# One core, eight batches of an adaLN block: new written-out step orders for five engines, and one wait less before a small load

## The chip, the cores and the metric

The kernel runs on one NeuronCore of a Trainium2 chip. The metric is the device time of one execution in microseconds (us). The time before is 694.33 us, the median of three runs (693.51 to 694.66).

## The reference

Eight batches of 1024 rows with 256 features, all float32. For each batch `b`:

```
mod = silu(c) @ wmod                       # six vectors of 256: sa, ca, ga, sb, cb, gb
ga, gb = sign * max(|.|, 0.25)
h = layernorm(x) * (1 + ca) + sa
x = x + ga * softmax((h*w_lhs) @ (h*w_rhs)^T) @ h      # 1024 x 1024 scores
h = layernorm(x) * (1 + cb) + sb
x = x + gb * (relu(h @ W1 + b1) @ W2 + b2)             # 256 -> 1024 -> 256
```

## The kernel before

A batch is cut into 8 tiles of 128 rows (two halves of 4). Every float32 product on TensorE is made of three: a value is split into a rounded part (`hi`) and a rest (`lo`), and hi*hi, hi*lo and lo*hi are added. TensorE so has the bulk of the work, and the other engines split, normalise, subtract the row maximum, exponentiate and turn blocks.

The attention of batch b and the feed-forward part (MLP) of batch b-1 run in one phase, together with the first layer norm of batch b+1. The phases are `before`, `first` (batch 0), `second` (batch 1), `middle` (a hardware loop over batches 2 to 6), `last` (batch 7) and `after` (the MLP of batch 7 alone). In each phase each engine (pe, act, dve, pool, sp) walks through a list of steps that is written out by hand as a string (`SECOND_STEPS` L70, `STEPS` L98, `LAST_STEPS` L126, `AFTER_STEPS` L151); `-` marks a step of batch b-1, `+` one of b+1. An engine runs its list strictly in order; between engines there are only semaphores. The steps that this text speaks of are:

- pe: `SC.n` the scores of row tile n (L631 to L633). They go by turns to two buffers, so SC.n waits until DVE has read SC.(n-2). `F.n` first MLP layer (L642 to L644, 6 matmuls of 512 columns), `G.n` second layer (L565, L566, L571, 12 of 256), `MB.h` spreads the row maxima of half h (L709), `AV.n` (L744 to L748, 24 matmuls) attention times values of row tile n, again in two buffers: AV.n waits until DVE has read AV.(n-2). G.0 waits for XG.3.
- dve: `SC.n` reads scores out with their maximum (L936 to L941), `ST`/`QT` turn blocks of them (L986, L994), `MX.h` row maxima, `SB.n` subtraction of the maximum (L972 to L983; it needs AV.(n-3) finished on pe), `SM.n` the rest `lo` of the exponentials (L1017), `AV.n` reads AV.n and adds it to x (L1023 to L1038, the read is L1034), `OUT.h` gates and adds the MLP result (L1132, L1136), `XG.k` writes x + gb*b2 to `x_mlp` (L1157), `VL.h` scales the values by the attention modulation `attn_mod` (L1144), `V.h` their rest (L1086), `B2`/`BH` turn normalised rows into blocks (L1096, L1097), `T2`/`TH` make the rests of the turned features (L1108; L1103, L1105).
- pool: `F.n` the rest of the hidden layer (L1194), `L1`/`L2` statistics (L1175 to L1178), `N1`/`N2` normalisation (L1185), `XC.k` adds to x (L1245).
- act: `F.n` relu and rounded part (L769, L773), `EX.n`, `SM.n` exponentials and their rounded part, `VN`, `V`, `T2`, `TH` likewise.
- sp, which issues all transfers: `AM` loads `attn_mod` (L450), `X0`/`X1` halves of x, `XT.h` the rows of the next batch's layer norm (`ln_t`, L489; XT.0 waits for B2.1), `S2`/`R2` and `SH`/`RH` store and reload blocks (L431, L438), `QW`/`QR`, `SW`/`SR` those of the scores, `GA` and `GB` two gate vectors, `O0`/`O1` the outputs (L501, L510). XG.2 waits until O1.0 and O1.1 of the batch before have landed, because it overwrites `x_mlp` (L1155).

The step that loads `gb_b2` and the step before it in the sp lists that has the same wait:

```
elif kind == "GB":
    wait(sp, xg_done, T // 2 * b)
    sp.dma_start(gb_b2[:], mod_rows[b, 3, :].partition_broadcast(P)).then_inc(gb_b2_in, 16)
elif kind == "X1":
    sp.wait_ge(xg_done, T // 2 * b)
    sp.dma_start(x_cur[:, HT:T, :], x_rows[b, 1]).then_inc(x_in[1], 16)
```

Of the kernel before, what the change touches and what calls it, by code (L numbers as in the profile page):

```python
# [148 lines left out]


AFTER_STEPS = {  # L151
    "pe": """
        F.0- F.1- F.2- F.3- F.4- F.5- G.0- G.1- G.2- G.3- F.6- G.4- G.5- F.7- F.8- F.9- F.10- G.6- G.7- F.11-
        F.12- G.8- G.9- F.13- G.10- F.14- F.15- G.11- G.12- G.13- GT.0-
    """,
    "act": """
        F.0- F.1- F.2- F.3- F.4- F.5- T2.1- F.6- F.7- F.8- F.9- F.10- F.11- F.12- F.13- F.14- F.15-
    """,
    "dve": """
        B2.1- XG.2- XG.3- T2.1- OUT.0- F.15- OT.0-  # L160
    """,
    "pool": """
        N2.1- F.0- F.1- F.2- F.3- F.4- F.5- F.6- F.7- F.8- F.9- F.10- F.11- F.12- F.13- F.14- OT.0-
    """,
    "sp": """
        S2.1- R2.1- GA.0- O0.0- O1.0- OT.2- OT.3-
# [1110 lines left out]
```

## Time and profile before

| quantity | value |
|---|---|
| time, median of three runs | 694.33 us |
| the profiled execution's own time | 694.33 us |
| its span, first to last instruction | 692.5 us |
| TensorE busy | 680.2 us (98%) |
| VectorE busy | 578.7 us (84%) |
| ScalarE busy | 428.2 us (62%) |
| GpSimd busy | 377.2 us (54%) |
| mean granted TensorE clock | 0.998 |

Busy is the sum of an engine's instructions over the span; the ends of matmuls are modelled, so TensorE's figure doesn't tell how much of its peak is used. What an engine waits for stands in brackets behind a row, with the instruction that released it. The distance between the starts of two matmuls is a better measure of a lost moment than the bracket: the bracket leaves out the time in which the earlier matmul still counts as running.

### The profile page before, as it was taken

Reading aid. Unit: us, or ns where it says so; the run is one execution under the profiler, and the core shown is the slowest. Engines: PE = TensorE matmul, PEld = TensorE weight load, DVE = VectorE, ACT = ScalarE, POOL = GpSimd, SP = SyncE. Lnnn points to the kernel's source line nnn. Section 1 sums busy time; section 2 is a strip of 40 time slices with the busy share of each in tenths; the row PEclk is TensorE's granted clock in tenths of the full one; section 3 lists DMA queues with packets and bytes.
Section 4 is the critical chain, followed back from the end, with each engine's and each line's share of the span. In section 5 each row is a group of like instructions: output and inputs, shape, how many; then the busy total and the mean of one; then the engine's idle time right before and its main releaser. Section 6 shows DMA issues by size and latency. Waiting matters only on the chain. (4 is left out here: it accounts for less than half of the span.)

```text
span 692.5 us, 13552 instructions
## 1 busy us (share of the span) xinstructions
PE 680.2 (98%) x4551; PEld 621.7 (90%) x4551; DVE 578.7 (84%) x1200; ACT 428.2 (62%) x625; POOL 377.2 (54%) x396
## 2 busy tenths in 40 slices
...
DMA packets 71744, 88.56 MB, mean 128 GB/s; under 512 B 6752, under 2 KB 62624, under 8 KB 71712
## 3 DMA queue, kind: packets, MB, share of 16 engines
...
HBM read 51.66 MB, written 36.47 MB: 127 GB/s over the span
## 5 line engine op out<-in xcount | busy, mean ns | idle before, releaser
L1194 POOL TENSOR_TENSOR hid_lo<-hid,hid_hi 128x512 fp32r<-128x512 f32 x127 | 176.5, 1397 | 184.9 <-ACT hid_hi L773 184.4
L769 ACT ACTIVATE hid<-col,b1T 128x512 f32<-128x512 f32 x128 | 86.4, 675 | 94.7 <-PE col L644 76.3
L565 PE MATMUL acc<-W2hi,hid_hi 128*128 128x256 f32 x480 | 117.4, 279 | 0.0
L566 PE MATMUL acc<-W2lo,hid_hi 128*128 128x256 f32 x480 | 116.7, 278 | 0.0
L744 PE MATMUL score<-V,Phi 128*128 128x258 f32 x448 | 109.4, 282 | 3.7 <-DVE x_cur L1034 3.1
L745 PE MATMUL score<-V,Phi 128*128 128x256 f32 x448 | 108.5, 281 | 0.0
L850 ACT ACTIVATE soft<-soft 128x1024 f32<-128x1024 f32 x56 | 59.2, 1058 | 70.2 <-DVE soft L983 48.6
L773 ACT ACTIVATE hid_hi<-hid 128x512 fp32r<-128x512 f32 x128 | 81.0, 633 | 34.8 <-PE acc L571 26.3
L642 PE MATMUL col<-h2hi,W1hi 128*128 128x512 f32 x256 | 101.3, 396 | 0.8 <-ACT hid L769 0.8
L644 PE MATMUL col<-h2hi,W1lo 128*128 128x512 f32 x256 | 100.9, 394 | 0.0
L643 PE MATMUL col<-h2lo,W1hi 128*128 128x512 f32 x256 | 100.4, 392 | 0.0
L565 PEld LDWEIGHTS acc<-W2hi,hid_hi 128*128 128x128 f32 x480 | 90.3, 188 | 1.4 <-issue 0.2
L566 PEld LDWEIGHTS acc<-W2lo,hid_hi 128*128 128x128 f32 x480 | 90.2, 188 | 1.3
L744 PEld LDWEIGHTS score<-V,Phi 128*128 128x128 f32 x448 | 85.0, 190 | 7.0 <-issue 5.9
L745 PEld LDWEIGHTS score<-V,Phi 128*128 128x128 f32 x448 | 84.1, 188 | 0.7
L571 PE MATMUL acc<-W2hi,hid_lo 128*128 128x256 f32 x480 | 77.1, 277 | 0.0
L1017 DVE TENSOR_TENSOR Plo<-soft,Phi 128x1024 fp32r<-128x1024 f32 x56 | 73.4, 1319 | 4.1 <-ACT Phi L866 4.1
L1245 POOL TENSOR_TENSOR x_cur<-x_cur,attn_mod 128x512 f32<-128x512 f32 x32 | 47.3, 1481 | 43.8 <-DVE ln_v L1144 31.8
L571 PEld LDWEIGHTS acc<-W2hi,hid_lo 128*128 128x128 f32 x480 | 64.5, 188 | 0.4
L748 PE MATMUL score<-V,Plo 128*128 128x258 f32 x448 | 63.3, 283 | 0.0
L866 ACT ACTIVATE Phi<-soft 128x1024 fp32r<-128x1024 f32 x56 | 57.7, 1051 | 0.7
L748 PEld LDWEIGHTS score<-V,Plo 128*128 128x128 f32 x448 | 57.3, 189 | 0.9 <-DVE Plo L1017 0.9
(154 smaller groups left out, 1477.3 us busy)
## 6 DMA issues: line engine op xcount, KB each, us to landing
...
```

The lines of the kernel that those rows point to most:

```text
L565: nc.tensor.matmul(o, hi, W2hi[:, it, :], start=(it == 0 and (apart or t % 2 == 0)), stop=False, skip_group_check=True)
L566: nc.tensor.matmul(o, hi, W2lo[:, it, :], start=False, stop=False, skip_group_check=True)
L571: last = nc.tensor.matmul(o, lo, W2hi[:, it, :], start=False, stop=(it == FT - 1), skip_group_check=True)
L642: nc.tensor.matmul(col[n % 2][:], W1hi[:, kk, tile], h2hi[:, kk, cols], start=(kk == 0), stop=False)
L643: nc.tensor.matmul(col[n % 2][:], W1hi[:, kk, tile], h2lo[:, kk, cols], start=False, stop=False)
L644: last = nc.tensor.matmul(col[n % 2][:], W1lo[:, kk, tile], h2hi[:, kk, cols], start=False, stop=(kk == DK - 1))
L744: nc.tensor.matmul(o, Phi[:, slot, t, :], V[:, t, 0:VW], start=(t == 0), stop=False)
L745: nc.tensor.matmul(o[:, 0:D], Phi[:, slot, t, :], V[:, t, VP:VP + D], start=False, stop=False)
L748: last = nc.tensor.matmul(o, Plo[:, slot, t, :], V[:, t, VP:VP + VW], start=False, stop=(t == T - 1))
L769: nc.scalar.activation(hid[:, n % 2, :], col[n % 2][:], ACT.Relu, bias=b1T[:, n % FT:n % FT + 1]).then_inc(col_read, 1)
L773: nc.scalar.activation(hid_hi[:, n % RING, :], hid[:, n % 2, :], ACT.Copy).then_inc(hid_hi_done, 1)
L1194: G.tensor_tensor(hid_lo[:, n % RING, :], hid[:, n % 2, :], hid_hi[:, n % RING, :].bitcast(F32), ALU.subtract).then_inc(hid_lo_done, 1)
```

## The change

The lists of `SECOND_STEPS`, `STEPS`, `LAST_STEPS` and `AFTER_STEPS` are replaced by others with the same steps in another order, for all five engines. `BEFORE_STEPS` and `FIRST_STEPS` stay. In the step GB the wait for `xg_done` is taken out; in each of the lists the step X1, which has that wait, stands ahead of GB. No instruction on tiles is added or removed. The middle phase (five of the eight batches) in full, and of the others the lists that the text speaks of:

```diff
 SECOND_STEPS = {
     "pe": """
-        SC.0 SC.1 F.0- SC.2 F.1- SC.3 F.2- SC.4 SC.5 G.0- F.3- F.4- SC.6 G.1- SC.7 F.5- G.2- G.3- G.4- MB.0
-        G.5- F.6- F.7- AV.0 F.8- F.9- G.6- F.10- G.7- AV.1 F.11- G.8- G.9- AV.2 G.10- MB.1 F.12- F.13- AV.3
-        F.14- G.11- AV.4 G.12- G.13- F.15- AV.5 AV.6 AV.7 G.14- G.15-
+        SC.0 SC.1 F.0- SC.2 SC.3 SC.4 F.1- F.2- SC.5 F.3- F.4- SC.6 SC.7 G.0- G.1- G.2- G.3- MB.0 F.5- G.4-
+        F.6- F.7- G.5- G.6- F.8- F.9- G.7- AV.0 F.10- AV.1 F.11- F.12- G.8- MB.1 AV.2 AV.3 F.13- G.9- G.10-
+        AV.4 G.11- F.14- G.12- AV.5 F.15- G.13- AV.6 G.14- G.15- AV.7
     """,
     "dve": """
-        SC.0 B2.1- XG.2- SC.1 SC.2 XG.3- VL.0 ST.0 SC.3 V.0 SC.4 SC.5 QT.0 L1.0+ ST.1 VL.1 ST.2 SC.6 SC.7
-        BH.0+ MX.0 ST.3 SB.0 T2.1- V.1 QT.1 SM.0 SB.1 AV.0 L1.1+ SM.1 SB.2 MX.1 OUT.0- AV.1 BH.1+ SM.2 SB.3
-        MX.2 TH.0+ SM.3 SB.4 SB.5 AV.2 XG.0 AV.3 SM.4 XG.1 SB.6 AV.4 B2.0 SM.5 SM.6 SB.7 TH.1+ AV.5 SM.7 AV.6
-        AV.7 OUT.1- T2.0
+        SC.0 ST.0 SC.1 B2.1- ST.1 SC.2 XG.2- VL.0 SC.3 SC.4 QT.0 L1.0+ XG.3- SC.5 V.0 SC.6 SC.7 T2.1- ST.2
+        QT.1 ST.3 MX.0 VL.1 SB.0 BH.0+ V.1 SB.1 SB.2 SM.0 L1.1+ OUT.0- MX.1 SM.1 SB.3 MX.2 AV.0 SM.2 AV.1
+        BH.1+ SB.4 SM.3 AV.2 SB.5 SB.6 AV.3 SM.4 TH.0+ SB.7 XG.0 SM.5 TH.1+ B2.0 AV.4 SM.6 AV.5 XG.1 SM.7 AV.6
+        OUT.1- AV.7 T2.0
     """,
     "sp": """
-        AM.0 S2.1- X1.0 XT.0+ R2.1- QW.0 SW.0 QR.0 SR.0 SH.0+ SW.1 XT.1+ SR.1 RH.0+ GA.0- QW.1 QR.1 SH.1+
-        O0.0- GB.0 RH.1+ S2.0 X0.0+ R2.0 O1.0- O1.1-
+        AM.0 S2.1- SW.0 XT.0+ R2.1- GA.0- QW.0 SR.0 QR.0 X1.0 SW.1 SR.1 QW.1 XT.1+ GB.0 QR.1 SH.0+ O0.0- RH.0+
+        SH.1+ RH.1+ S2.0 R2.0 O1.0- O1.1- X0.0+
     """,
...
 STEPS = {
     "pe": """
-        SC.0 SC.1 F.0- F.1- SC.2 F.2- SC.3 F.3- SC.4 G.0- SC.5 F.4- SC.6 F.5- SC.7 G.1- G.2- F.6- G.3- MB.0
-        F.7- G.4- F.8- G.5- G.6- G.7- F.9- F.10- F.11- G.8- AV.0 AV.1 G.9- G.10- G.11- F.12- MB.1 F.13- AV.2
-        AV.3 G.12- F.14- AV.4 AV.5 G.13- AV.6 G.14- F.15- AV.7 G.15-
+        SC.0 SC.1 F.0- SC.2 SC.3 F.1- F.2- SC.4 F.3- SC.5 G.0- SC.6 G.1- SC.7 F.4- G.2- F.5- F.6- G.3- G.4-
+        MB.0 F.7- G.5- G.6- AV.0 F.8- G.7- F.9- F.10- AV.1 MB.1 F.11- AV.2 F.12- AV.3 F.13- G.8- G.9- G.10-
+        AV.4 G.11- F.14- AV.5 G.12- AV.6 F.15- G.13- G.14- G.15- AV.7
     """,
     "act": """
-        F.0- VN.0 F.1- F.2- V.0 F.3- T2.1- F.4- F.5- VN.1 F.6- EX.0 SM.0 F.7- V.1 F.8- L1.0+ F.9- EX.1 EX.2
-        F.10- SM.1 F.11- TH.0+ EX.3 SM.2 SM.3 EX.4 F.12- F.13- EX.5 SM.4 SM.5 TH.1+ EX.6 SM.6 MC.0 F.14- EX.7
+        F.0- VN.0 F.1- F.2- V.0 F.3- T2.1- F.4- VN.1 F.5- V.1 F.6- EX.0 SM.0 F.7- EX.1 SM.1 EX.2 F.8- F.9-
+        L1.0+ EX.3 SM.2 F.10- SM.3 TH.0+ EX.4 SM.4 F.11- F.12- EX.5 SM.5 F.13- EX.6 SM.6 TH.1+ F.14- EX.7 MC.0
         SM.7 F.15- T2.0
     """,
     "dve": """
-        B2.1- SC.0 SC.1 XG.2- VL.0 ST.0 XG.3- SC.2 ST.1 SC.3 QT.0 SC.4 ST.2 V.0 ST.3 SC.5 L1.0+ T2.1- SC.6
-        SC.7 QT.1 MX.0 BH.0+ SB.0 VL.1 SM.0 SB.1 V.1 OUT.0- SB.2 MX.1 L1.1+ SM.1 AV.0 SB.3 AV.1 MX.2 BH.1+
-        SM.2 SM.3 SB.4 TH.0+ SB.5 AV.2 AV.3 SM.4 XG.0 SM.5 SB.6 AV.4 XG.1 B2.0 SM.6 SB.7 TH.1+ AV.5 SM.7 AV.6
-        AV.7 OUT.1- T2.0
+        XG.2- SC.0 XG.3- SC.1 B2.1- SC.2 ST.0 ST.1 SC.3 VL.0 QT.0 SC.4 L1.0+ SC.5 ST.2 ST.3 SC.6 V.0 SC.7
+        BH.0+ QT.1 T2.1- VL.1 MX.0 V.1 SB.0 SB.1 SB.2 SM.0 L1.1+ MX.1 SM.1 SB.3 MX.2 AV.0 SM.2 SB.4 OUT.0-
+        AV.1 SM.3 SB.5 TH.0+ BH.1+ AV.2 SM.4 AV.3 SB.6 SB.7 SM.5 XG.0 XG.1 SM.6 AV.4 B2.0 TH.1+ AV.5 SM.7 AV.6
+        OUT.1- AV.7 T2.0
     """,
     "pool": """
-        N2.1- XC.0 F.0- F.1- F.2- F.3- L1.0+ F.4- N1.0+ F.5- F.6- F.7- XC.1 F.8- F.9- XC.2 F.10- L1.1+ N1.1+
-        F.11- XC.3 F.12- F.13- L2.0 N2.0 F.14- F.15- L2.1
+        N2.1- F.0- XC.0 F.1- F.2- L1.0+ N1.0+ F.3- XC.1 F.4- F.5- XC.2 F.6- F.7- F.8- XC.3 F.9- F.10- L1.1+
+        N1.1+ F.11- L2.0 F.12- N2.0 F.13- F.14- F.15- L2.1
     """,
     "sp": """
-        AM.0 GA.0- S2.1- XT.0+ R2.1- SW.0 QW.0 X1.0 QR.0 SR.0 SW.1 SH.0+ QW.1 SR.1 XT.1+ RH.0+ GB.0 QR.1 O0.0-
-        SH.1+ RH.1+ S2.0 R2.0 X0.0+ O1.0- O1.1-
+        XT.0+ AM.0 X1.0 S2.1- R2.1- QW.0 GA.0- SW.0 QR.0 GB.0 SR.0 QW.1 SH.0+ SW.1 XT.1+ QR.1 SR.1 RH.0+ O0.0-
+        SH.1+ RH.1+ S2.0 R2.0 O1.0- X0.0+ O1.1-
     """,
 }
 LAST_STEPS = {
     "pe": """
-        SC.0 SC.1 F.0- SC.2 F.1- F.2- SC.3 G.0- G.1- F.3- F.4- SC.4 SC.5 G.2- G.3- SC.6 F.5- SC.7 F.6- F.7-
-        MB.0 G.4- G.5- F.8- G.6- AV.0 F.9- F.10- G.7- F.11- AV.1 AV.2 G.8- F.12- MB.1 G.9- AV.3 G.10- F.13-
-        AV.4 G.11- F.14- G.12- F.15- AV.5 AV.6 G.13- AV.7 G.14- G.15-
+        SC.0 SC.1 SC.2 F.0- SC.3 F.1- SC.4 F.2- SC.5 F.3- SC.6 SC.7 G.0- F.4- G.1- G.2- F.5- F.6- G.3- G.4-
+        MB.0 F.7- G.5- F.8- F.9- AV.0 G.6- G.7- F.10- AV.1 F.11- AV.2 MB.1 AV.3 F.12- G.8- F.13- G.9- G.10-
+        F.14- AV.4 G.11- G.12- AV.5 F.15- G.13- AV.6 G.14- G.15- AV.7
     """,
     "dve": """
-        SC.0 B2.1- ST.0 XG.2- SC.1 XG.3- ST.1 SC.2 ST.2 SC.3 QT.0 VL.0 SC.4 V.0 ST.3 SC.5 VL.1 SC.6 T2.1- SC.7
-        MX.0 SB.0 QT.1 V.1 SM.0 SB.1 AV.0 SM.1 SB.2 OUT.0- SM.2 SB.3 MX.1 MX.2 SM.3 AV.1 AV.2 SB.4 AV.3 SM.4
-        SB.5 SB.6 B2.0 SM.5 SB.7 AV.4 SM.6 XG.0 AV.5 SM.7 XG.1 AV.6 T2.0 AV.7 OUT.1-
+        SC.0 SC.1 ST.0 XG.2- VL.0 SC.2 SC.3 ST.1 XG.3- QT.0 B2.1- SC.4 SC.5 V.0 VL.1 ST.2 SC.6 ST.3 SC.7 T2.1-
+        MX.0 QT.1 V.1 SB.0 SB.1 SM.0 MX.1 SB.2 SB.3 MX.2 SM.1 AV.0 AV.1 SM.2 SM.3 OUT.0- AV.2 AV.3 SB.4 SB.5
+        SB.6 SM.4 B2.0 SM.5 SB.7 AV.4 XG.0 SM.6 SM.7 XG.1 AV.5 T2.0 AV.6 OUT.1- AV.7
     """,
...
 AFTER_STEPS = {
     "pe": """
-        F.0- F.1- F.2- F.3- F.4- F.5- G.0- G.1- G.2- G.3- F.6- G.4- G.5- F.7- F.8- F.9- F.10- G.6- G.7- F.11-
-        F.12- G.8- G.9- F.13- G.10- F.14- F.15- G.11- G.12- G.13- GT.0-
+        F.0- F.1- F.2- G.0- F.3- F.4- G.1- G.2- F.5- G.3- F.6- F.7- G.4- G.5- G.6- F.8- F.9- G.7- G.8- F.10-
+        F.11- F.12- G.9- F.13- G.10- F.14- F.15- G.11- G.12- G.13- GT.0-
     """,
     "dve": """
-        B2.1- XG.2- XG.3- T2.1- OUT.0- F.15- OT.0-
+        XG.2- XG.3- B2.1- T2.1- OUT.0- F.15- OT.0-
     """,
     "pool": """
-        N2.1- F.0- F.1- F.2- F.3- F.4- F.5- F.6- F.7- F.8- F.9- F.10- F.11- F.12- F.13- F.14- OT.0-
+        F.0- F.1- N2.1- F.2- F.3- F.4- F.5- F.6- F.7- F.8- F.9- F.10- F.11- F.12- F.13- F.14- OT.0-
     """,
...
@@ -452,7 +452,6 @@
                     elif kind == "GA":
                         sp.dma_start(gb_all[:], mod_rows[f, 2, :].partition_broadcast(P)).then_inc(gb_in, 16)
                     elif kind == "GB":
-                        wait(sp, xg_done, T // 2 * b)
                         sp.dma_start(gb_b2[:], mod_rows[b, 3, :].partition_broadcast(P)).then_inc(gb_b2_in, 16)
                     elif kind == "S2":
                         store_blocks(ph.turn(b, "T2", n))
```

## Rows read from the trace of the kernel before

**Rows 1.** the page, first part: busy us, share of the span, instructions

```profile
PE 680.2 (98%) x4551; PEld 621.7 (90%) x4551; DVE 578.7 (84%) x1200; ACT 428.2 (62%) x625; POOL 377.2 (54%) x396
```

**Rows 2.** the waits of TensorE, 71 to 700: us, times, longest

```profile
PE score L744 <- DVE x_cur L1034: 3.1, 5, 0.6
PE col L642 <- ACT hid L769: 0.8, 1, 0.8
PE score L631 <- DVE S L941: 0.7, 1, 0.7
PE score L744 <- ACT Phi L866: 0.5, 1, 0.5
```

**Rows 3.** busy us by stretch (PE, PEld, DVE, ACT, POOL), clock: batch 4

```profile
316.70:398.70 82.00, 81.29 (x563) 75.18 (x562) 74.09 (x153) 54.81 (x80) 47.14 (x48) 1.00 0.48 141
```

**Rows 4.** timeline of TensorE: start, us, what, idle before it

```profile
311.14 0.39 PE L643 MATMUL col<-h2lo,W1hi 128*128 128x512 f32 x1
311.37 0.40 PE L644 MATMUL col<-h2hi,W1lo 128*128 128x512 f32 x1
312.37 0.38 PE L744 MATMUL score<-V,Phi 128*128 128x258 f32 x1 [0.61 <-DVE x_cur L1034]
312.59 0.28 PE L745 MATMUL score<-V,Phi 128*128 128x256 f32 x1
312.71 0.28 PE L744 MATMUL score<-V,Phi 128*128 128x258 f32 x1
...
324.11 0.40 PE L644 MATMUL col<-h2hi,W1lo 128*128 128x512 f32 x1
324.61 0.50 PE L631 MATMUL score<-Rhi,Lhi 128*128 128x512 f32 x1
```

**Rows 5.** timeline of VectorE, late in batch 4: SB.7, then TH.1

```profile
389.63 0.54 DVE L972 TENSOR_TENSOR soft<-S,score 128x384 f32<-128x384 f32 x1
...
390.89 0.74 DVE L1103 SCALAR_TENSOR_TENSOR Llo<-featT,wl,Lhi 128x512 fp32r<-128x512 f32 x1
```

**Rows 6.** line L1034 (DVE's read of AV): ns min/median/max, first and last start, form

```profile
L1034 DVE SCALAR_TENSOR_TENSOR x_cur<-score,inv_sum,x_cur x56: 483/484/489, 107.9 to 642.8; 128x256 f32<-128x256 f32 x56
```

**Rows 7.** line L1017 (DVE's SM): the same columns

```profile
L1017 DVE TENSOR_TENSOR Plo<-soft,Phi x56: 1181/1224/2332, 105.2 to 636.9; 128x1024 fp32r<-128x1024 f32 x56
```

**Rows 8.** timeline of VectorE where batch 4 begins

```profile
319.61 1.53 DVE L1108 TENSOR_TENSOR h2lo<-featT,h2hi 128x512 fp32r<-128x512 f32 x2
322.26 0.71 DVE L1096 STREAM_TRANSPOSE blocks<-ln_t 128x512 f32<-128x512 f32 x1 [1.12 <-POOL ln_t L1185]
...
323.49 1.05 DVE L936 TENSOR_SCALAR_CACHE_REDUCE S<-score 128x896 f32<-128x896 f32 x1
...
325.49 0.69 DVE L1157 TENSOR_TENSOR x_mlp<-x_cur,gb_b 128x512 f32<-128x512 f32 x1
326.09 1.67 DVE L1144 SCALAR_TENSOR_TENSOR ln_v<-ln_v,rs,attn_mod 128x256 f32<-128x256 f32 x4
...
328.30 1.38 DVE L1157 TENSOR_TENSOR x_mlp<-x_cur,gb_b 128x512 f32<-128x512 f32 x1
```

**Rows 9.** the page, DMA issues: count, KB each, median us to landing

```profile
out<-x_mlp SPq DMA_DIRECT2D x15, 256.0 KB, 2.2
...
attn_mod<-mod_rows SPq DMA_DIRECT2D x8, 256.0 KB, 3.8
```

**Rows 10.** timeline of GpSimd, the same stretch

```profile
319.00 3.10 POOL L1185 TENSOR_SCALAR ln_t<-x_cur,nm,rs 128x256 f32<-128x256 f32 x4 [0.22 <-POOL rs L1178]
327.84 1.29 POOL L1245 TENSOR_TENSOR x_cur<-x_cur,attn_mod 128x512 f32<-128x512 f32 x1 [5.74 <-DVE ln_v L1144]
```

**Rows 11.** timeline of SyncE's queue, the same stretch: when a transfer is issued

```profile
318.52 1.71 SPq L510 DMA_DIRECT2D out<-x_mlp  x2
320.76 0.37 SPq L450 DMA_DIRECT2D attn_mod<-mod_rows  x1
```

**Rows 12.** timeline of GpSimd, beginning of the phase after

```profile
646.03 2.17 POOL L1185 TENSOR_SCALAR ln_t<-x_cur,nm,rs 128x256 f32<-128x256 f32 x4 [0.21 <-issue]
```

More of the change, by code:

```diff
@@ L75 @@
+        AV.4 G.11- F.14- G.12- AV.5 F.15- G.13- AV.6 G.14- G.15- AV.7
     """,
     "act": """
-        VN.0 F.0- L1.0+ V.0 F.1- F.2- VN.1 F.3- F.4- T2.1- V.1 F.5- EX.0 SM.0 F.6- F.7- EX.1 SM.1 F.8- F.9-
-        EX.2 TH.0+ SM.2 F.10- F.11- EX.3 SM.3 F.12- F.13- EX.4 EX.5 SM.4 MC.0 TH.1+ EX.6 SM.5 SM.6 F.14- EX.7
-        F.15- SM.7 T2.0
+        VN.0 F.0- F.1- F.2- V.0 T2.1- F.3- F.4- MC.0 L1.0+ VN.1 V.1 F.5- EX.0 F.6- F.7- SM.0 EX.1 EX.2 F.8-
+        F.9- SM.1 SM.2 F.10- EX.3 SM.3 TH.0+ F.11- EX.4 SM.4 F.12- EX.5 SM.5 TH.1+ EX.6 F.13- EX.7 SM.6 SM.7
@@ L80 @@
+        F.14- F.15- T2.0
     """,
     "dve": """
-        SC.0 B2.1- XG.2- SC.1 SC.2 XG.3- VL.0 ST.0 SC.3 V.0 SC.4 SC.5 QT.0 L1.0+ ST.1 VL.1 ST.2 SC.6 SC.7
-        BH.0+ MX.0 ST.3 SB.0 T2.1- V.1 QT.1 SM.0 SB.1 AV.0 L1.1+ SM.1 SB.2 MX.1 OUT.0- AV.1 BH.1+ SM.2 SB.3
-        MX.2 TH.0+ SM.3 SB.4 SB.5 AV.2 XG.0 AV.3 SM.4 XG.1 SB.6 AV.4 B2.0 SM.5 SM.6 SB.7 TH.1+ AV.5 SM.7 AV.6
-        AV.7 OUT.1- T2.0
+        SC.0 ST.0 SC.1 B2.1- ST.1 SC.2 XG.2- VL.0 SC.3 SC.4 QT.0 L1.0+ XG.3- SC.5 V.0 SC.6 SC.7 T2.1- ST.2
@@ L86 @@
+        QT.1 ST.3 MX.0 VL.1 SB.0 BH.0+ V.1 SB.1 SB.2 SM.0 L1.1+ OUT.0- MX.1 SM.1 SB.3 MX.2 AV.0 SM.2 AV.1
+        BH.1+ SB.4 SM.3 AV.2 SB.5 SB.6 AV.3 SM.4 TH.0+ SB.7 XG.0 SM.5 TH.1+ B2.0 AV.4 SM.6 AV.5 XG.1 SM.7 AV.6
+        OUT.1- AV.7 T2.0
     """,
     "pool": """
-        N2.1- F.0- XC.0 F.1- F.2- XC.1 L1.0+ F.3- N1.0+ F.4- F.5- F.6- F.7- XC.2 F.8- L1.1+ F.9- N1.1+ XC.3
-        F.10- F.11- F.12- F.13- L2.0 N2.0 F.14- F.15- L2.1
+        N2.1- XC.0 F.0- L1.0+ F.1- F.2- F.3- N1.0+ F.4- F.5- F.6- F.7- F.8- F.9- F.10- L1.1+ N1.1+ XC.1 F.11-
```

17 lines of the change are left out of this document (7 added, 10 removed).

## The prediction

> **What bounds the kernel now.** First the page: TensorE is busy 680.2 us, 98% of the span [rows 1]. No work is removed, so only TensorE's lost moments can be won. Second its waits from 71 us on [rows 2]: one reason occurs five times, once in each middle batch; three others occur once. Third the stretch of one middle batch [rows 3]: it takes 82.0 us, with VectorE busy 74.1, so VectorE is 8 us from being the bound itself. Fourth TensorE's timeline, by distances between starts [rows 4]. Two 512-column matmuls start 0.23 apart, two of 256 columns 0.12. Ahead of AV.7 the distance is 1.00, so 0.77 is lost where the bracket shows 0.61; ahead of SC.2 (324.61) it is 0.50, so 0.27 is lost where no bracket stands. A middle batch so loses 1.04 us of 82.0. For the single waits I add the same 0.16 to each: 0.86 in the second phase, 0.66 in the last, 0.96 in the phase after. Together 5 x 1.04 + 2.48 = 7.7 us: the most that new orders of the same work behind 71 us can win. What they can lose has no such ceiling.
>
> For the sums: an F step is 6 x 0.23 = 1.4 us of TensorE, a G step 12 x 0.12 = 1.4, an AV step 24 x 0.12 = 2.9. Times below are counted from TensorE's first matmul of a batch (316.7 for batch 4) and the period without losses is 82.0 - 1.04 = 81.0.
>
> **The wait ahead of AV.7 (five times 0.77).** AV.7 needs VectorE's read of AV.5. Between the end of AV.5 and AV.7 TensorE had G.13, AV.6, G.14, F.15: 3 x 1.4 + 2.9 = 7.1 us. Now it has G.12, AV.6, F.15, G.13, G.14, G.15: 9.9 us. VectorE still does TH.1 (four instructions of 0.74, the first in [rows 5]) ahead of AV.5, but XG.1, SM.6 and SB.7 no longer lie between AV.4 and AV.5 on its list. 2.8 us more time against 0.77 missing: this one goes.
>
> What is late next is AV.6, which needs the read of AV.4. From the end of AV.4 TensorE now has G.11, F.14, AV.5, G.12: 7.1 us. VectorE has SB.7 (which itself needs AV.4 finished; 1.26 by the starts in [rows 5]), SM.5 1.2, XG.0 and XG.1 0.6 each, SM.6 1.2, and the read of AV.4, 0.48 [rows 6] and 0.2 for the reciprocal ahead of it: 5.6 us. SM.6 takes between 1.2 and 2.3 [rows 7], so up to 6.7. VectorE reaches SB.7 by my count some 0.9 after AV.4's end, which gives 6.5 to 7.6 against 7.1. New loss: 0 to 0.5, taken as 0.3.
>
> **The wait ahead of SC.2 (five times 0.27).** VectorE stood 1.12 us for N2.1 ahead of B2.1, and SC.0 behind it was read late [rows 8]. Now XG.2, SC.0, XG.3, SC.1 stand ahead of B2.1. F.1 is moved behind SC.3, so TensorE wants SC.0's read at 7.65 - 1.4 = 6.25. AV.7 is now the last PE step; its own step on VectorE, reciprocal, read and two statistics, is some three times the 0.48 of the read [rows 6] and ends at 1.45, T2.0 (1.5, [rows 8]) at 2.95. XG.2 adds a wait: O1.1 must have landed. OUT.1 now stands before AV.7, G.15 being finished 2.9 us before the phase's end, so O1.1 is issued at about 0.4 and lands 2.2 later [rows 9], at 2.6; with X0's 512 KB now issued between O1.0 and O1.1 I allow 3.8, the landing time of the small load in [rows 9], which gives 4.2. Queued behind XG.2 on VectorE are SC.0 (then TensorE's SC.2), XG.3 and X1 on SyncE. XG.2 0.6 and SC.0 1.0 [rows 8] end at 4.6 to 5.8 against 6.25. The 0.27 goes; the bounds of the new loss are 0 and 0.3.
>
> XG.2 and XG.3 now run beside N2.1 on GpSimd. XG.3 took 1.38 instead of 0.69 where it started at 328.30, inside XC.0 (327.84 to 329.13) [rows 8, 10]: it ended 0.55 after XC.0 did, as if it had waited. One N2.1 instruction lasts 3.10/4 = 0.78, so one such wait puts SC.0's read at 5.4 to 6.6, the upper bound 0.35 late. The Trainium skill says it as a rule (SBUF — State Buffer, Who interferes with whom): a VectorE instruction with both inputs in SBUF and a GpSimd instruction that reads SBUF exclude each other, the second one waiting till the first is through. By that rule the move costs up to 0.35 a batch, without it nothing; the trace agrees in the row cited.
>
> **SyncE's order (AM behind XT.0).** AM was issued at 320.76 - 316.7 = 4.1 [rows 11], VL.0 used it at 9.4 [rows 8]. XT.0 now stands first, and waits until B2.1 has run. N2.1 ends about 1.45 later than before (5.4, [rows 10]), at 6.9; B2.1 ends at about 8.3; AM is issued at 8.9 and lands at 12.7 (3.8, [rows 9]). In the new list VL.0 comes after two SC, two ST and another SC, at about 12.2. So VectorE waits 0.5 here, behind it QT.0, SC.4 and XC.0 on GpSimd. TensorE meets SC.6 (which needs SC.4 read) later than that; the next meeting is MB.0, then AV.0, where my count leaves 0.3 to 0.5 us of slack. Taken as nothing; bounds 0 and 2.0, the latter if the 512 KB of XT.0 and X1 around it double its landing time.
>
> The wait removed in GB costs nothing now: X1, ahead of it, has the same wait. 0, and no bound other than 0.
>
> **Second phase.** The 0.86 is SC.5 waiting for SC.3's read behind VL.0; the new list puts one F step more between SC.3 and SC.5, and it goes. But G.0 to G.3 now run together and MB.0 comes two steps (2.8 us) earlier on TensorE, while VectorE's work ahead of MX.0 is as long as it was (VL.1 and BH.0 out; T2.1, QT.1 and ST.3 in). The 2.8 must come out of VectorE's idle time, of which a whole batch has 8 [rows 3]. New loss 0 to 2.0, taken as 1.0. Net: 0.1 lost.
>
> **Last phase.** AV.6 came directly behind AV.5 and waited for EX/SM.6 (0.66). Now F.15 and G.13 stand between, 2.8 us. It goes; 0.2 for new ones, bounds 0 and 1. Net 0.5 won.
>
> **Phase after.** N2.1 held GpSimd for 2.17 [rows 12] ahead of F.0's rest, ACT's F.2 and so TensorE's F.4 (0.96). It is moved behind F.0 and F.1, and goes. But G.0 now comes after three F steps, at 4.2, and needs XG.3: O1.1 lands at 2.6, two XG of 0.69 to 1.38 [rows 8] end at 4.0 to 5.4. Loss 0 to 1.2, taken as 0.5. Net 0.5 won. Moved N2.1 delays the turned features for F.8, which has 0 to 1 us left by the same kind of count.
>
> **Sum.** 5 x (1.04 - 0.3) - 0.1 + 0.5 + 0.5 = 4.6. The profiled execution's own time is 694.33, 1.8 outside the span, and it is also the median: 694.33 - 4.6 = 689.7.
>
> **Rivals.**
> 1. All losses go and none comes: 694.33 - 7.7 = 686.6. For it: each new wait above is at 0 at its lower bound, and VectorE has 8 us idle. Against it: VectorE then has 7.
> 2. The gains come back elsewhere (AV.6 0.5 and SC.2 0.35 a batch, and 0.2 at AV.0): 693.7 to 694.3, no change.
> 3. Slower: the attention modulation. If AM lands 2.0 later than the 12.7 counted, VL.0, SC.4, SC.6's reads and finally MX.0 and SM.0 on VectorE are 2.5 late, 0.5 of it is slack, and TensorE stands 2.0 at MB.0 or AV.0 in each middle batch: 5 x (2.0 + 0.3 - 1.04) = 6.3 lost, less 0.9 won at the ends: 699.7. From a landing at about 13.9 on (1.2 later) it outweighs the gain; at that point the time is 694 to 695. For it: three more transfers are issued within 2 us of AM. Against it: they stand behind it, except one.
>
> **How the numbers follow.** My forecast 0.48 (687.5 to 692.5), rival 1 0.20, rival 2 0.14, rival 3 0.18. A measurement of this kernel tells 0.2% (1.4 us) from no change. Faster: 0.48 + 0.20 = 0.68; same 0.14; slower 0.18. The range goes from rival 1's time to 695.5, just into rival 3; beyond that less than 0.15 is left, below it some 0.03.
>
> **What would show it.** Right: in the middle batches no wait of TensorE ahead of AV.7 for L1034, no distance over 0.23 ahead of SC.2, a period of 81.0 to 81.5, and the largest wait ahead of AV.6. VectorE's first XG.2 waits for a transfer or not at all. No wait in the phase after for L769. Wrong: a wait of TensorE for L1013 or for Plo at AV.0 (rival 3), VL.0 held by the `attn_mod` transfer for over 1.7 us; or a period of 82 with the lost time spread over new places (rival 2). A lower granted clock anywhere behind 71 us would be outside all of these.

## The result and the profile after

The changed kernel takes 735.43 us (median of four runs, 734.62 to 737.37) against 693.92 (four runs): ratio 1.060, 95% interval 1.0578 to 1.0627. I had forecast 689.7, 686.5 to 695.5. The time is outside the range and on the other side.

The page and the waits of TensorE after, to be laid beside [rows 1] and [rows 2]. Lines behind the removed wait have numbers lower by one (L708 is MB, L747 the last third of AV, L570 that of G, L1012 the row maximum, L1016 SM, L1143 VL):

```profile
PE 694.4 (94%) x4551; PEld 629.5 (85%) x4551; DVE 595.5 (81%) x1200; ACT 431.6 (59%) x625; POOL 374.5 (51%) x396
```

```profile
PE score L708 <- DVE row_max L1012: 17.3, 5, 3.8
PE score L747 <- DVE Plo L1016: 7.6, 6, 3.8
PE score L630 <- DVE S L932: 2.9, 5, 0.9
PE col L641 <- ACT hid L768: 1.9, 1, 1.9
PE col L641 <- DVE h2lo L1107: 1.5, 1, 1.5
PE score L630 <- DVE x_cur L1033: 1.4, 5, 0.3
...
PE score L743 <- DVE x_cur L1033: 0.7, 1, 0.7
```

The wait ahead of AV.7, 3.1 us in five places, is gone (the 0.7 that is left lies in the second phase, ahead of AV.6). In its place stands MB.0, waiting for the row maxima, 17.3 us.

By the starts of SC.0 the phases last, second to after: before 81.8, 81.6, 82.0, 82.0, 82.0, 82.0, 81.2, 45.4; now 84.9, 92.0, 89.3, 89.0, 89.9, 89.8, 82.7, 46.5. These are the profiled executions, 694.33 and 739.14 us. Of the 46.0 us that the phases lost (what lies ahead of them was 1.2 shorter in the second trace), 40.4 lie in the five middle batches. Batch 4, the stretch that answers [rows 3], and 3.1 us of it; columns as there. Its SC.0 starts at 336.24, 0.26 ahead of the first row's window, and the times "into the batch" below are counted from there:

```profile
336.50:425.50 89.00, 83.72 (x562) 76.78 (x561) 76.69 (x153) 55.51 (x81) 46.41 (x48) 0.98 0.44 130
372.30:375.40 3.10, 3.10 (x13) 2.80 (x12) 3.10 (x9) 1.68 (x3) 1.28 (x1) 0.51 1.13 218
```

SyncE's queue at the beginning of that batch (compare [rows 11]): start, length of the issue, what:

```profile
337.59 0.38 SPq L509 DMA_DIRECT2D out<-x_mlp  x1
346.26 0.38 SPq L488 DMA_DIRECT2D ln_t<-x  x1
346.83 0.36 SPq L450 DMA_DIRECT2D attn_mod<-mod_rows  x1
347.39 0.37 SPq L491 DMA_DIRECT2D x_cur<-x  x1
347.81 0.50 SPq L431 DMA_DIRECT2D block_rows<-blocks  x1
355.25 1.76 SPq L438 DMA_DIRECT2D blocks<-block_rows  x4
```

VectorE in the same batch (compare [rows 8]), with its three waits for transfers and what stood between:

```profile
341.39 0.72 DVE L1156 TENSOR_TENSOR x_mlp<-x_cur,gb_b 128x512 f32<-128x512 f32 x1 [1.36 <-DMA out<-x_mlp]
...
352.74 1.67 DVE L1143 SCALAR_TENSOR_TENSOR ln_v<-ln_v,rs,attn_mod 128x256 f32<-128x256 f32 x4 [3.65 <-DMA attn_mod<-mod_rows]
...
367.31 2.67 DVE L1143 SCALAR_TENSOR_TENSOR ln_v<-ln_v,rs,attn_mod 128x256 f32<-128x256 f32 x4
...
370.89 0.18 DVE L1012 TENSOR_REDUCE row_max<-part_max 128x4 f32<-128x16 f32 x1
...
378.46 0.69 DVE L979 TENSOR_TENSOR soft<-S,score 128x512 f32<-128x512 f32 x1 [2.86 <-DMA S<-score_blocks]
```

And TensorE where it pays:

```profile
371.12 0.65 PE L708 MATMUL score<-ident,row_max 128*128 128x128 f32 x4 [3.49 <-DVE row_max L1012]
...
372.30 0.59 PE L641 MATMUL col<-h2hi,W1hi 128*128 128x512 f32 x1
372.69 0.63 PE L642 MATMUL col<-h2lo,W1hi 128*128 128x512 f32 x1
373.12 0.63 PE L643 MATMUL col<-h2hi,W1lo 128*128 128x512 f32 x1
```

```profile
380.34 1.10 PE L747 MATMUL score<-V,Plo 128*128 128x258 f32 x7 [0.95 <-DVE Plo L1016]
```

The rows are to be read as one chain. B2.1 ends at 346.1, XT.0 is issued and only then, behind it, AM: 10.6 us into the batch (4.1 before). Four transfers, 1.8 MB together, are issued within 2 us. The modulation lands 5.8 us after its issue. VL.0 has stood 3.65 us by then, and so has everything behind it on VectorE. The block store takes 7.4 us instead of 2.6, SyncE stands at R2.1 till 355.25, and the reloads of the scores (QR, SR) are issued behind that. The row maxima are ready at 371.1, MB.0 was wanted at 367.5. Then SB.2 stands for the last reloaded scores, SM.0 behind it, and AV.0 in the middle of its matmuls. After the 3.5 us of standing the granted clock is at 0.51 in the 3.1 us of the second row, the lower of TensorE's two levels (1.2 GHz): 512-column matmuls start 0.39 to 0.43 apart, not 0.23. The whole stretch at that level is 3.4 us long:

```profile
372.34:375.75 3.41, 3.41 (x15) 3.12 (x14) 3.26 (x9) 2.01 (x2) 1.28 (x1) 0.50 1.12 220
```

By start distances batch 4 lost 3.65 ahead of MB.0, 1.11 in AV.0, 0.70 ahead of SC.6, 0.44 in SC.0, 0.2 ahead of F.6, together 6.1; the period is 8.0 over 81.0, and half the clock for 3.4 us is 1.7 of the 1.9 that remain.

### The profile page after: what moved, and what is told of

Its sections match the earlier page's. It is cut to its first block, busy times and chain, and to the rows that moved or that the text cites. A ratio compares the mean times of both kernels' runs of the same rounds, so it can differ in the third digit from the quotient of the medians.

```text
span 737.3 us, 13552 instructions
## 1 busy us (share of the span) xinstructions
PE 694.4 (94%) x4551; PEld 629.5 (85%) x4551; DVE 595.5 (81%) x1200; ACT 431.6 (59%) x625; POOL 374.5 (51%) x396
## 4 chain that ended last, share of the span: by engine, by line
DVE 29%; PE 21%; DMA 20%; issue 13%; POOL 9%; SPq 3%; ACT 3%; DVEq 1%; POOLq 0%; ACTq 0%
POOL ln_t L1184 5%; DMA score_blocks<-stage 4%; DVE Llo L1102 4%; DMA attn_mod<-mod_rows 3%; DMA S<-score_blocks 3%; DVE Plo L1016 3%; DVE Rlo L1104 3%; PE score L747 3%; DMA block_rows<-blocks 2%; DVE stats L1035 2%; DVE x_cur L1033 2%; DMA out<-x_mlp 2%; DVE acc L1131 2%; PE col L641 2%; PE col L643 2%
## 5 line engine op out<-in xcount | busy, mean ns | idle before, releaser
L1193 POOL TENSOR_TENSOR hid_lo<-hid,hid_hi 128x512 fp32r<-128x512 f32 x127 | 172.8, 1367 | 181.5 <-ACT hid_hi L772 179.5
L564 PE MATMUL acc<-W2hi,hid_hi 128*128 128x256 f32 x480 | 119.8, 283 | 0.0
L565 PE MATMUL acc<-W2lo,hid_hi 128*128 128x256 f32 x480 | 119.4, 282 | 0.0
L641 PE MATMUL col<-h2hi,W1hi 128*128 128x512 f32 x256 | 104.4, 408 | 3.6 <-ACT hid L768 1.9
L642 PE MATMUL col<-h2lo,W1hi 128*128 128x512 f32 x256 | 102.7, 401 | 0.0
L564 PEld LDWEIGHTS acc<-W2hi,hid_hi 128*128 128x128 f32 x480 | 92.7, 193 | 2.3
L565 PEld LDWEIGHTS acc<-W2lo,hid_hi 128*128 128x128 f32 x480 | 92.5, 193 | 2.3
L1016 DVE TENSOR_TENSOR Plo<-soft,Phi 128x1024 fp32r<-128x1024 f32 x56 | 76.9, 1376 | 5.8 <-ACT Phi L865 5.8
L570 PE MATMUL acc<-W2hi,hid_lo 128*128 128x256 f32 x480 | 78.0, 280 | 1.0 <-POOL hid_lo L1193 0.8
L1244 POOL TENSOR_TENSOR x_cur<-x_cur,attn_mod 128x512 f32<-128x512 f32 x32 | 43.0, 1347 | 70.0 <-DVE ln_v L1143 57.8
L747 PE MATMUL score<-V,Plo 128*128 128x258 f32 x448 | 63.4, 284 | 7.6 <-DVE Plo L1016 7.6
L570 PEld LDWEIGHTS acc<-W2hi,hid_lo 128*128 128x128 f32 x480 | 65.6, 191 | 2.0 <-POOL hid_lo L1193 1.9
L747 PEld LDWEIGHTS score<-V,Plo 128*128 128x128 f32 x448 | 57.3, 189 | 8.8 <-DVE Plo L1016 8.8
L630 PE MATMUL score<-Rhi,Lhi 128*128 128x512 f32 (+2 forms) x168 | 58.6, 349 | 5.8 <-DVE S L932 2.9
```

Of the source, the lines that this page charges most:

```text
L564: nc.tensor.matmul(o, hi, W2hi[:, it, :], start=(it == 0 and (apart or t % 2 == 0)), stop=False, skip_group_check=True)
L565: nc.tensor.matmul(o, hi, W2lo[:, it, :], start=False, stop=False, skip_group_check=True)
L570: last = nc.tensor.matmul(o, lo, W2hi[:, it, :], start=False, stop=(it == FT - 1), skip_group_check=True)
L641: nc.tensor.matmul(col[n % 2][:], W1hi[:, kk, tile], h2hi[:, kk, cols], start=(kk == 0), stop=False)
L642: nc.tensor.matmul(col[n % 2][:], W1hi[:, kk, tile], h2lo[:, kk, cols], start=False, stop=False)
L747: last = nc.tensor.matmul(o, Plo[:, slot, t, :], V[:, t, VP:VP + VW], start=False, stop=(t == T - 1))
```

## Experiments

Comparisons are with the kernel before on the same chip. Where nothing else is said, the list in a diff is that of the middle phase (`STEPS`), and its lines are cut down to the steps that moved.

**e1.** The changed kernel with the old SyncE list in the middle phase.

```diff
 STEPS "sp"
-XT.0+ AM.0 X1.0 S2.1- R2.1- QW.0 GA.0- SW.0 QR.0 GB.0 SR.0 QW.1 SH.0+ SW.1 XT.1+ QR.1 SR.1 RH.0+ O0.0- ...
+AM.0 GA.0- S2.1- XT.0+ R2.1- SW.0 QW.0 X1.0 QR.0 SR.0 SW.1 SH.0+ QW.1 SR.1 XT.1+ RH.0+ GB.0 QR.1 O0.0- ...
```

> The changed kernel with SyncE's list of the middle phase as it was (AM.0 first, XT.0 behind S2.1, SR and QR in the old places); everything else is changed. Theory A (SyncE's order: XT.0 with its wait stands ahead of the attention modulation, and four transfers of 1.8 MB are issued together, so that VL.0 and the turned scores come late): the middle batches go from 89 to 92 us back to 81 to 83, VL.0 waits for nothing, and the time is 696 to 702 us. Theory B (the orders of VectorE and TensorE themselves: XG.2 waits for the output to land, MB.0 is wanted too early): the wait ahead of MB.0 stays above 2 us, and the time is above 718 us.

Measured: 702.98 us, ratio 1.013 (1.0113 to 1.0147). Middle batches 82.5 to 83.1. VL.0 waits for nothing:

```profile
333.05 1.67 DVE L1143 SCALAR_TENSOR_TENSOR ln_v<-ln_v,rs,attn_mod 128x256 f32<-128x256 f32 x4
```

Theory A holds, though the time is 1.0 us over its range: SyncE's middle list alone is worth 32 of the 41 us. What is left is 1.0 a middle batch (MB.0 still waits, 8.3 us in all) and some 4 us in the other phases.

**e2.** The changed kernel, one step moved.

```diff
 STEPS "sp"
-XT.0+ AM.0 X1.0 S2.1- ...
+AM.0 XT.0+ X1.0 S2.1- ...
```

> The changed kernel with one step moved: in the middle phase AM.0 stands ahead of XT.0. Theory A1 (the late attention modulation carries the loss): VL.0's wait of 3.7 us goes, the wait ahead of MB.0 (3.9 us) goes with it and so does the half clock behind it (1.7 us), 5 batches: 700 to 708 us. Theory A2 (the loss is carried by the bunch of transfers that holds back the block store, behind which SyncE waits before it may reload the turned scores): MB.0's wait shrinks by under 2 us, SB.2 still waits for score_blocks, 718 to 732 us.

Measured: 730.99 us (726.96 to 736.9), ratio 1.055 (1.0486 to 1.0617). A1's range (700 to 708) failed, A2's (718 to 732) holds the median. VL.0's wait is gone and MB.0's shrank from 17.3 to 9.2 us in all, but most of the time comes back one step later, at AV.0, through SB.2:

```profile
PE score L747 <- DVE Plo L1016: 16.2, 6, 3.7
PE score L708 <- DVE row_max L1012: 9.2, 6, 2.1
```

```profile
369.86 0.69 DVE L979 TENSOR_TENSOR soft<-S,score 128x512 f32<-128x512 f32 x1 [4.04 <-DMA S<-score_blocks]
```

**e3.** The kernel before with the changed SyncE list in the middle phase (the diff of e1 turned round).

> The kernel before with SyncE's list of the middle phase as changed; everything else as before. Theory A: SyncE's order alone is enough: VL.0 waits 3 us or more for the attention modulation, the time rises to 712 to 735 us. Theory B: under 702 us.

Measured: 716.48 us, ratio 1.032 (1.0304 to 1.0342), middle batches 86.4 to 89.7. The list harms the old orders of the other engines too, by 22.6 us. VL.0 waits 10.6 us in five places, 2.7 at most, a little less than theory A wanted.

**e4.** The changed kernel with VectorE's old list in the middle phase (B2.1 first, VL.0 earlier, T2.1 earlier).

```diff
 STEPS "dve"
-XG.2- SC.0 XG.3- SC.1 B2.1- SC.2 ST.0 ST.1 SC.3 VL.0 ...
+B2.1- SC.0 SC.1 XG.2- VL.0 ST.0 XG.3- SC.2 ST.1 SC.3 ...
```

> The changed kernel with VectorE's list of the middle phase as it was (B2.1 first, VL.0 behind XG.2). Theory A: XT.0 is released some 2 us earlier, but the modulation still lands behind it and VL.0 stands earlier on the list: the loss stays, 720 to 745 us. Theory B: 695 to 705 us.

Measured: 850.27 us, ratio 1.224 (1.2208 to 1.2269), 112 us a middle batch, the waits spread over F, SC, G, MB.0 and two places in the AV steps. Both expectations missed it by over 100 us. Putting VectorE's old list back doesn't take the loss away, it adds to it: one list of five can't be put back here without the others. What part VectorE's new list has in the loss this run doesn't tell.

**e5.** The modulation late, the bunch broken up.

```diff
 STEPS "sp"
-XT.0+ AM.0 X1.0 S2.1- R2.1- QW.0 GA.0- SW.0 QR.0 ...
+XT.0+ S2.1- R2.1- AM.0 QW.0 GA.0- SW.0 X1.0 QR.0 ...
```

> The changed kernel with two steps moved in SyncE's list of the middle phase: S2.1 and R2.1 directly behind XT.0, AM.0 behind them and X1.0 behind SW.0. So the attention modulation is as late as in the changed kernel (issued after R2.1), but the block store has only XT.0 ahead of it. Theory A1 (the modulation carries the loss): VL.0 still waits 3 us or more, MB.0 still 3 us or more: 722 to 740 us. Theory A2 (the bunch carries it): S2.1 lands within 3 to 4 us instead of 7, the turned scores come 3 us earlier, SB.2 waits for nothing: under 715 us. If each alone is enough to cost most of the time, both this and the kernel with AM.0 first stay within 10 us of the changed kernel.

Measured: 763.74 us, ratio 1.102 (1.100 to 1.1037). That is outside both ranges. AM is now held back by R2.1's wait as well and lands later than in the changed kernel, so the two causes aren't cleanly parted; but the dose is larger and so is the loss: VL.0 waits 7.8 us instead of 3.65, and batch 4 takes 95.5 instead of 89.0. SB.2 still waits for reloaded scores (15.5 us in five places).

```profile
363.94 1.67 DVE L1143 SCALAR_TENSOR_TENSOR ln_v<-ln_v,rs,attn_mod 128x256 f32<-128x256 f32 x4 [7.80 <-DMA attn_mod<-mod_rows]
```

**e11.** The smallest dose, in the kernel before.

```diff
 STEPS "sp"
-AM.0 GA.0- S2.1- XT.0+ R2.1- ...
+GA.0- S2.1- XT.0+ AM.0 R2.1- ...
```

> The kernel before with one step moved: in SyncE's middle list AM.0 stands behind XT.0 instead of first. Theory (one transfer that stands behind a waiting one is enough): the modulation is issued some 3.5 us later, VL.0 waits 1.5 to 3 us, TensorE then waits at SC.4 or SC.5 or MB.0: 698 to 712 us. Rival (it is the number of transfers issued together that matters, VectorE's 8 us of idle a batch take this up): 693 to 696 us.

Measured: 711.68 us (707.0 to 713.2), ratio 1.023 (1.0193 to 1.0264). One 256 KB load, put behind the block store and XT.0, which wait for B2.1, costs 17.5 us. Part of that is the clock: the one execution at a mean granted clock of 1.0 took 707.0, the three at 0.988 to 0.993 took 711.4 to 713.2. In batch 4 VL.0 stands 3.4 us, TensorE 2.2 at SC.4:

```profile
331.41 0.65 SPq L450 DMA_DIRECT2D attn_mod<-mod_rows  x1
```

```profile
336.23 1.67 DVE L1144 SCALAR_TENSOR_TENSOR ln_v<-ln_v,rs,attn_mod 128x256 f32<-128x256 f32 x4 [3.37 <-DMA attn_mod<-mod_rows]
```

```profile
340.73 0.44 PE L631 MATMUL score<-Rhi,Lhi 128*128 128x384 f32 x1 [2.20 <-DVE S L936]
```

VectorE's 8 us of idle a batch did not take it up: all but 1.1 of them lie after this point.

**e9.** e2, and the second bunch reordered.

```diff
 STEPS "sp"
-XT.0+ AM.0 ... SR.0 QW.1 SH.0+ SW.1 XT.1+ QR.1 SR.1 RH.0+ ...
+AM.0 XT.0+ ... SR.0 SW.1 QW.1 SR.1 SH.0+ QR.1 XT.1+ RH.0+ ...
```

> The changed kernel (735 us) with AM.0 first in SyncE's middle list (alone: 731 us), and in the second bunch the reload of the scores' second half moved up: SW.1, QW.1, SR.1, SH.0, QR.1, XT.1 in place of QW.1, SH.0, SW.1, XT.1, QR.1, SR.1. Theory now: SyncE's order costs at two places one behind the other, VL.0 (attention modulation) and SB.2 (the scores of half 1, whose reload SR.1 stands behind four other transfers); taking away one shows the other. Then SB.2 waits for nothing and the middle batches take 83 to 84 us as with the old list: 702 to 708 us. Rival (the first bunch of four transfers and R2.1 behind it still hold SyncE): 718 us or more.

Measured: 722.22 us, ratio 1.041 (1.0378 to 1.0435). The theory's range (702 to 708) failed, the rival's (718 or more) holds. SB.2 no longer waits and the mean granted clock is 0.998, but XT.1, moved back, is late, and VectorE's L1.1 stands for it:

```profile
DVE stats L1056 <- DMA ln_t<-x: 23.6, 7, 4.3
```

So a third transfer becomes the late one. The first bunch still holds SyncE, as the rival had it: the reload R2.1 goes out 17.2 us into the batch, in e1 at 12.4. MB.0 waits 14.1 us in ten places.

**e13.** The consumer moved, no transfer.

```diff
 STEPS "dve"
-... SC.3 VL.0 QT.0 SC.4 L1.0+ SC.5 ST.2 ST.3 SC.6 ...
+... SC.3 QT.0 SC.4 L1.0+ SC.5 ST.2 ST.3 VL.0 SC.6 ...
```

> The changed kernel with VL.0 on VectorE's middle list moved behind QT.0, SC.4, L1.0, SC.5, ST.2 and ST.3; no transfer is moved. Theory C (the order of the list turns one late transfer into a wait of everything behind it): VL.0's wait for the modulation, 3.7 us, is filled with work, MB.0's wait falls from 3.9 to under 2 us, the half clock behind it goes, and the time is 705 to 722 us, SB.2's wait remaining. Rival (the values are needed that early anyway: XC.0 and with it GpSimd's F.1 stand behind VL.0, G.1 needs it): the wait moves to G.1 or to SC.6, 728 us or more.

Measured: 745.73 us, ratio 1.075 (1.0729 to 1.0762). Theory C falls, its rival holds: VectorE doesn't wait for the modulation any more, but VL.0 now runs 19.4 us into the batch instead of 16.5, XC.0 on GpSimd waits for VL.0, F.1 stands behind XC.0, and G.1 then stands in the middle of its matmuls.

```profile
364.38 0.74 PE L570 MATMUL acc<-W2hi,hid_lo 128*128 128x256 f32 x4 [3.96 <-POOL hid_lo L1193]
```

**e12.** The wait in GB put back.

```diff
+                        wait(sp, xg_done, T // 2 * b)
```

> The changed kernel with the wait in GB put back. X1.0, ahead of it in each list, has the same wait, so nothing changes: 730 to 741 us.

Measured: 740.91 us (two runs, 740.5 and 741.4), middle batches 88.8 to 91.7, not measured side by side with the 735.4. With the wait back the loss is still there, so its removal isn't the cause. Whether the 5 us between them is the wait or the spread of this kernel (the profiled execution of the changed kernel took 739.1, e2 spread over 10 us) two runs don't tell.

**e6.** e1 with MX.0 ahead of T2.1 and VL.1.

```diff
 STEPS "dve"
-QT.1 T2.1- VL.1 MX.0 V.1 ...
+QT.1 MX.0 T2.1- VL.1 V.1 ...
```

> The kernel with SyncE's old middle list (703.0 us), and MX.0 on VectorE ahead of T2.1 and VL.1 in the middle phase. There TensorE waited 1.7 us a batch ahead of MB.0. If only MX.0's place was wrong, that wait goes and nothing comes: 703.0 - 5 x 1.7 = 694.5 us. If VectorE is simply behind (T2.1 and VL.1 took 2.6 and 2.7 us there instead of 1.3 and 1.7 beside GpSimd's work), the wait moves to AV.0, which needs SM.0: 700 to 703 us.

Measured: 706.76 us (703.97 to 710.5), ratio 1.021 (1.0182 to 1.0238), above both ranges. The wait moves from MB.0 to AV.0:

```profile
PE score L743 <- ACT Phi L865: 7.7, 6, 1.5
```

The execution with the trace took 703.97; the slower ones have a mean granted clock down to 0.990. Even in the trace the clock fell once, behind the last of five like waits of 1.45 us:

```profile
522.57 0.39 PE L743 MATMUL score<-V,Phi 128*128 128x258 f32 x1 [1.45 <-ACT Phi L865]
```

```profile
523.27:526.69 3.42, 3.42 (x19) 3.42 (x18) 3.42 (x10) 3.25 (x4) 1.30 (x1) 0.50 0.09 20
```

**e15.** e1 with XC.1 on GpSimd later.

```diff
 STEPS "pool"
-... F.3- XC.1 F.4- F.5- XC.2 ...
+... F.3- F.4- F.5- XC.1 XC.2 ...
```

> The kernel with SyncE's old middle list (703.0 us) and XC.1 on GpSimd behind F.5 in the middle phase. If GpSimd's reads hold VectorE up where both inputs lie in SBUF, T2.1 and VL.1 (5.3 us together there, 3.0 in the kernel before) become 0.6 to 1.3 us shorter, MB.0's wait of 1.7 us as much, and the time is 697 to 701 us. If GpSimd's F.4 and F.5 take XC.1's place beside them, or MB.0 waits for something else: 702 to 704 us.

Measured: 703.95 us, ratio 1.0145 (1.0129 to 1.0161); MB.0's wait as before. VectorE's two steps and GpSimd's beside them:

```profile
345.57 1.84 DVE L1107 TENSOR_TENSOR h2lo<-featT,h2hi 128x512 fp32r<-128x512 f32 x2
347.34 3.72 DVE L1143 SCALAR_TENSOR_TENSOR ln_v<-ln_v,rs,attn_mod 128x256 f32<-128x256 f32 x4
```

```profile
347.79 1.57 POOL L1193 TENSOR_TENSOR hid_lo<-hid,hid_hi 128x512 fp32r<-128x512 f32 x1 [1.52 <-ACT hid_hi L772]
349.31 1.46 POOL L1244 TENSOR_TENSOR x_cur<-x_cur,attn_mod 128x512 f32<-128x512 f32 x1
```

T2.1 and VL.1 took 2.57 and 2.70 in e1, now 1.84 and 3.72: the sum stays (5.3 and 5.6). Four such instructions alone take 1.67. The clash is moved, not removed, and the time is in the second range (702 to 704).

**e7.** The kernel before with the two waits of a middle batch attacked directly.

```diff
 STEPS "dve"
-B2.1- SC.0 ... SB.7 TH.1+ AV.5 SM.7 ...
+SC.0 B2.1- ... SB.7 AV.5 TH.1+ SM.7 ...
```

> The kernel before with two steps of VectorE's middle list moved and nothing else: AV.5 ahead of TH.1, SC.0 ahead of B2.1. If TensorE's two lost moments of a middle batch (0.77 ahead of AV.7, 0.27 ahead of SC.2) were all that could be won there, and cost nothing elsewhere: 693.9 - 5.2 = 688.7 us. If VectorE's lateness only moves on (TH.1's rests late for the next SC.0): 692 to 695 us.

Measured: 691.90 us (ten runs), ratio 0.9977 (0.9967 to 0.9986), nearer to "moves on" (692 to 695) than to 688.7. Middle batches 81.6. SC.2's 0.27 went. AV.7's 0.77 went too, and 0.74 came back inside the same AV.7, which now waits for SM.7 (behind TH.1):

```profile
312.78 0.99 PE L748 MATMUL score<-V,Plo 128*128 128x258 f32 x6 [0.58 <-DVE Plo L1017]
```

**e8.** e7 with three more moves.

```diff
 SECOND_STEPS "dve"
-VL.0 ST.0 SC.3 V.0
+VL.0 SC.3 ST.0 V.0
 LAST_STEPS "act"
-EX.7 SM.6
+SM.6 EX.7
 AFTER_STEPS "pool"
-N2.1- F.0- F.1- F.2- ...
+F.0- F.1- N2.1- F.2- ...
```

> The kernel before with the two moves of the previous run and three more: in the phase after GpSimd's N2.1 behind F.1 (the changed kernel's list for that engine and phase), in the last phase ACT's SM.6 ahead of EX.7, in the second phase VectorE's SC.3 ahead of ST.0. Each removes one wait of TensorE of 0.5 to 0.8 us (0.7 to 1.0 by starts): 688.7 - 2.3 = 686.4 us if all go and none comes; 688 to 690 if one of them moves on.

Measured: 693.27 us, ratio 0.9989 (0.9976 to 1.0001), above both forecasts (686.4, and 688 to 690). Second phase 82.2 (82.8 in e7), last 80.4 (81.2), but the phase after 48.0 (45.2): G.0 waits 2.1 for XG.3, which stands behind the delayed B2.1, and the clock falls behind this wait. Of the ten executions, three at a granted clock of 1.0 took 691.0 to 691.4, seven at 0.998, which is what one stretch of 3.4 us at half clock makes of the mean, took 692.8 to 694.4. Whether the clock falls behind such a wait so differs from one execution to the next, and costs about 2 us when it does.

**e10.** e8 with the changed VectorE list of the phase after.

```diff
 AFTER_STEPS "dve"
-B2.1- XG.2- XG.3- T2.1- ...
+XG.2- XG.3- B2.1- T2.1- ...
```

> The kernel before with the five moves of e8 (693.3 us) and VectorE's list of the phase after as in the changed kernel (XG.2 and XG.3 ahead of B2.1). In e8 the phase after took 48.0 us instead of 45.2, G.0 waiting 2.1 us for XG.3 behind the later N2.1 and B2.1. If that order was all: the phase takes 44.2 to 45 us and the time is 689 to 690.5 us. If XG.2 now waits for the output to land, or the turned features come too late for F.8: 691 to 693 us.

Measured: 695.49 us, ratio 1.0008 (0.9991 to 1.0024), above both ranges; the phase takes 49.3. XG.2 waits 2.5 us for the output to land, and the turned features come 3.3 us too late for F.8:

```profile
663.37 0.50 PE L642 MATMUL col<-h2hi,W1hi 128*128 128x512 f32 x1 [3.32 <-DVE h2lo L1108]
```

**e14.** e7 with the first two of e8's three further moves.

```diff
 SECOND_STEPS "dve"
-VL.0 ST.0 SC.3 V.0
+VL.0 SC.3 ST.0 V.0
 LAST_STEPS "act"
-EX.7 SM.6
+SM.6 EX.7
```

> The kernel before with four steps moved: AV.5 ahead of TH.1 and SC.0 ahead of B2.1 (VectorE, middle), SC.3 ahead of ST.0 (VectorE, second), SM.6 ahead of EX.7 (ACT, last); the phase after as before. From the stretches seen so far: 694.0 - 5 x 0.35 - 0.6 - 0.8 = 690.9 us, 690 to 691.5.

Measured: 690.69 us (five runs), ratio 0.9954 (0.994 to 0.9968), as expected: four moved steps, 3.1 us faster than the kernel before on the same chip, and faster than the changed kernel.

## Why the prediction was wrong

The mechanism that decided was in the text as rival 3, with 0.18, and its place was right: AM behind XT.0, VL.0, then MB.0 and AV.0. It was priced at 2.0 us a batch there, and stood at nothing in the forecast itself. Four terms were mis-sized.

1. **The step "SyncE's order", taken as nothing.** I had AM issued at 8.9 and landed at 12.7. It was issued at 10.6. AV.7's step on VectorE stood behind OUT.1 and ended at 2.6, not 1.45, so N2.1 ended at 8.4, not 6.9. And XG.2 waited for the output till 5.1 (I allowed 4.2 at most), so that SC.1's read, ahead of B2.1, ended at 8.5. B2.1 with XT.0 stood behind both. Then AM landed 5.8 after its issue, at 16.4, not 3.8 after it. The 3.8 was the landing time in the kernel before, where two 256 KB stores go out ahead of this load and a 128 KB load behind it; I knew the bunch of transfers and used it for the upper bound only. VectorE reached VL.0 at 12.9 and began it at 16.5. e1 gives 32 us back with the old list, and e11 pays 17.5 for AM's place alone in the old orders.
2. **What else stands in the queue.** I counted AM and left out SyncE's own wait at R2.1. The block store behind three others took 7.4, and R2.1 went out 19.0 into the batch instead of 9.8. The reloads QR.0 and SR.0 were issued 5.1 and 5.7 later than in the kernel before, SR.1 at 34.9, where e1 has it at 26.7. e2 shows what that costs: with AM in time most of the loss stays, at SB.2. In the text SB.2 did not occur as a user of SR.1; it needs it, as MX.1 does. e9 then shows the next one.
3. **The slack.** "0.3 to 0.5 at MB.0 and AV.0" had no row for VectorE's steps between. Without any late transfer (e1) MB.0 still waits 1.7 us a batch, where T2.1 and VL.1 take 5.3 us, not 3.0: I weighed the clash with GpSimd for XG.2 and XG.3 only, and those then ran at 0.7; GpSimd's N2.1 beside them took 3.2, not the 2.17 of [rows 12]. That the 2.3 us more make this wait is argued, not shown: e6 and e15, which moved one side each, only moved the wait or the clash.
4. **The price of a stall.** Rival 3 ended at 699.7, with 2.0 us a batch. Behind waits of 3.5 to 3.8 us TensorE ran at half clock for 3.4 us, once in each of batches 2 to 5 and for 6.8 us in batch 6, 1.7 us lost each time; in e1, whose longest wait there is 1.7 us, the mean granted clock is 1.0. I wrote that a lower clock would be outside all cases.

Point by point for the rest. AV.7: right, the wait for AV.5's read is gone in the middle batches. AV.6's new wait of 0.3: none appeared in the middle batches (in e1 either), but one of 0.7 in the second phase. SC.2: its 0.27 is gone in e1, but SC.0's right half waits 0.44 a batch for AV.7's read, AV.7 now being last; I had passed over that term. O1.1 lands 3.7 after its issue, which came at 1.35; I had 3.8 and 0.4, so the landing time was right and the issue 0.95 off. The wait in GB: no loss explained by its removal, its exact worth open. Second phase: forecast 0.1 lost, measured 3.1 (84.9 for 81.8; the old lists of this phase took 82.8 in e3, e7 and e11, so 2.1 to 3.1). The wait of SC.5 went as forecast, and MB.0, where I put the new loss, doesn't wait; two G steps wait for GpSimd instead and AV.6 for VectorE. Last: forecast 0.5 won, 1.5 lost. After: 0.5 won, 1.1 lost, by F.8 waiting 1.52 for T2.1, which I had left "0 to 1 us". Without SyncE's list the forecast would still have been 13.3 us too low (e1: 702.98), and slower than the kernel before by 9.1, nearly all of it the new waits at MB.0 and the losses of the outer phases.

e7 and e14 show what the winnable 7.7 us were worth: 1.7 and 3.1. In e6, e7, e8 and e10 a move against one wait uncovered another just behind. Open is how the 40 us divide exactly between the modulation and the reloads: e5 was meant to part them and didn't, and e2 and e9 show that taking one away uncovers the next. Open too is how the 9 us of e1 divide between the lists of the other four engines; only e4 tried to part them.
